# Expert weights loaded once per layer into SBUF, and copied tile by tile into the ring by VectorE

## The reference

```python
gate_logits = x @ Wg + bg
top_vals, top_idx = jax.lax.top_k(gate_logits, TOP_K)      # TOP_K = 2 of 8
...
h = jnp.einsum('td,edh->eth', xf, W0) + b0[:, None, :]      # gated: 128 -> 512, twice
g = jax.nn.silu(jnp.einsum('td,edh->eth', xf, W1) + b1[:, None, :])
y = jnp.einsum('eth,ehd->etd', h * g, W2) + b2[:, None, :]  # 512 -> 128
...
    h = jax.nn.gelu(flat @ W1[e] + b1[e], approximate=False)   # ungated: 128 -> 512, once
    out = out + combine[:, e:e + 1] * (h @ W2[e] + b2[e])
```

## Time and profile before

| | |
|---|---|
| median of three runs | 1117.88 us (1116.94 to 1121.6) |
| the profiled execution's own time | 1118.18 us |
| its span, first to last instruction | 1116.4 us |
| mean granted TensorE clock | 0.863 of full speed |
| busy: PE, PEld, DVE, ACT, POOL | 797.7, 680.7, 538.7, 445.3, 433.3 us |
| chain that ended last | PE 58%, DVE 24%, issue 7%, DMA 4%, ACT 3%, POOL 3% |
| DMA queue q1 (SyncE's and the other hardware queues) | 134.03 MB |

### The profile page before, as it was taken

The page is one execution under the profiler, slowest core; times in us unless marked ns, Lnnn a source line. Parts: engine busy times, 40 slices in busy tenths (PEclk is TensorE's granted clock), DMA queues, the critical chain, the costliest instruction groups (busy, mean ns, idle before and its releaser), DMA issues.

```text
span 1116.4 us, 17251 instructions
## 1 busy us (share of the span) xinstructions
PE 797.7 (71%) x5220; PEld 680.7 (61%) x5220; DVE 538.7 (48%) x1633; ACT 445.3 (40%) x1259; POOL 433.3 (39%) x448
## 2 busy tenths in 40 slices
PE   0579997378989865899974767774177877777750
PEld 0479997267777645798973566664034555666650
DVE  4734444777656537344447521113889543310117
ACT  0045554144445320455550145553087331265540
POOL 1256663022222210565631066663453210466631
PEclk9999999698989985799995579997598885699995
DMA  4559985362513003598954247775000011477752
GB/s 110 131 177 293 291 271 180 95 152 55 124 42 82 2 9 121 179 291 279 276 174 132 94 114 213 211 207 144 1 0 1 1 30 35 136 212 211 210 162 65
DMA packets 79082, 153.77 MB, mean 138 GB/s; under 512 B 11082, under 2 KB 54035, under 8 KB 78992
## 3 DMA queue, kind: packets, MB, share of 16 engines
q1 hardware_dynamic: 69008, 134.03, 40.6%
q0 software_dynamic: 9984, 18.65, 6.1%
HBM read 134.21 MB, written 20.25 MB: 138 GB/s over the span
## 4 chain that ended last, share of the span: by engine, by line
PE 58%; DVE 24%; issue 7%; DMA 4%; ACT 3%; POOL 3%; SPq 1%; another core or an unknown queue 0%; POOLq 0%; ACTq 0%; DVEq 0%
PE bank L521 14%; PE bank L512 12%; PE bank L509 8%; PE bank L945 2%; DVE stats L281 2%; PE bank L528 2%; PE bank L460 2%; PE bank L935 2%; DVE oh_b L623 2%; PE bank L497 2%; DVE sh_tok L675 2%; PE bank L1270 2%; DVE x_tok L675 2%; PE bank L908 1%; PE bank L477 1%
## 5 line engine op out<-in xcount | busy, mean ns | idle before, releaser
L512 PE MATMUL bank<-xt,weights 128*128 128x128 f32 x1248 | 249.8, 283 | 27.5 <-ACT xt L411 16.6
L521 PE MATMUL bank<-hid,weights 128*128 128x128 f32 x1248 | 245.1, 279 | 11.0 <-ACT hid L422 8.2
L348 POOL DMA_INDIRECT xg<-xn_rows,gidx x156 | 153.1, 982 | 238.7 <-DVE gidx L629 129.9
L512 PEld LDWEIGHTS bank<-xt,weights 128*128 128x128 f32 x1248 | 196.5, 199 | 33.9 <-ACT xt L411 20.3
L521 PEld LDWEIGHTS bank<-hid,weights 128*128 128x128 f32 x1248 | 191.1, 194 | 15.3 <-ACT hid L422 9.5
L355 POOL DMA_INDIRECT y_rows<-yo,sidx x156 | 157.1, 1007 | 91.8 <-issue 56.3
L650 DVE SCALAR_TENSOR_TENSOR hid<-bank,weights,act_ring 128x128 f32<-128x128 f32 x312 | 108.9, 349 | 139.5 <-ACT act_ring L422 83.2
L422 ACT ACTIVATE act_ring<-bank,weights 128x128 f32<-128x128 f32 x312 | 115.8, 371 | 111.1 <-PE bank L512 96.5
L657 DVE COPY yo<-bank 128x128 f32<-128x128 f32 x156 | 44.6, 286 | 213.2 <-remote 127.6
L422 ACT ACTIVATE hid<-bank,weights 128x128 f32<-128x128 f32 x312 | 110.6, 372 | 79.8 <-PE bank L521 51.1
L509 PE MATMUL bank<-xt,weights 128*128 128x128 f32 x624 | 128.8, 289 | 5.8 <-issue 2.5
(11 more groups left out here) (220 smaller groups left out, 1341.8 us busy)
## 6 DMA issues: line engine op xcount, KB each, us to landing
weights<-glu_pack SPq DMA_DIRECT2D x78, 772.5 KB
weights<-mlp_pack SPq DMA_DIRECT2D x78, 514.5 KB
v_sb<-v_rows SPq DMA_DIRECT2D x48, 180.0 KB, 6.5
y_in<-y_rows SPq DMA_DIRECT2D x32, 256.0 KB, 5.0
xn_rows<-xm_tok SPq DMA_DIRECT2D x16, 256.0 KB, 2.2
v_rows<-vd SPq DMA_DIRECT2D x16, 256.0 KB, 2.8
xg<-xn_rows,gidx POOLq DMA_INDIRECT x156
y_rows<-yo,sidx POOLq DMA_INDIRECT x156
```

What stands on the lines that cost most here:

```text
L348: pool.indirect_dma_start(out=xg[:, slot, :], out_offset=None, in_=xn_dram.ap()[:, :], in_offset=bass.IndirectOffsetOnAxis(ap=gidx[:, j:j ...
L512: nc.tensor.matmul(banks[k % 4][:, 0:TS], wt[:, slot, o:o + P], xt[:, j % 2, :], start=True, stop=True).then_inc(sem(st + "_up"), 1)
L521: nc.tensor.matmul(YD[j % 2], wt[:, j % WSLOTS, o:o + P], hid[:, k % 4, :], start=c == 0, stop=c == HC - 1).then_inc(sem(st + "_dn"), 1)
```

## The change

At a layer's front SyncE now issues eight DMAs that load all eight experts' sets into a new SBUF tensor `all_w`. They are behind the four stores of `xn_rows` and wait for nothing else. SyncE no longer reads `te_i`. VectorE has a generator `tile_weights(j)`: it waits for the ring slot, reads the expert into a register of its own, and copies the set out of `all_w` in pieces of 512, 512 and 521 columns (gated) or 512 and 517 (ungated), one piece per step. The ring has four slots in place of five. Three sets are copied before the tile loop; in the loop, tile j carries the copies of tile j+3, one piece behind each `chunk(j, c)`. TensorE waits for one semaphore `_tile_w`.

```diff
--- before.py
+++ after.py
@@ -24,7 +24,7 @@
 NTILE = (2 * NT * P + E * (TS - 1)) // TS
 NA = -(-NTILE // 2) * 2
 SLOTS_BASE = 2 * NT * P
-WSLOTS, XSLOTS, PIECES, LAG = 5, 6, 4, 3
+WSLOTS, XSLOTS, PIECES, LAG = 4, 6, 4, 3
 BEHIND = 3
 
 
@@ -78,9 +78,7 @@
     if kind in ("glu", "mlp"):
         per = {"_up": HC * NTILE, "_act": HC * NTILE, "_hid": HC * NTILE, "_dn": HC * NTILE, "_gT": NTILE, "_xt": NTILE,
                "_ysb": NTILE, "_yT": NTILE, "_yo": NTILE, "_xn_out": 16 * NBLK, "_logits": 1, "_scattered": 16 * NTILE, "_incl": 1, "_offs": 1,
-               "_te": 1, "_onehot": PIECES, "_table": 1, "_idx": 1, "_gap": 1, "_tanh": 1}
-        for i in range(WSLOTS):
-            per[f"_w_in{i}"] = 16 * turns_of(WSLOTS, i)
+               "_te": 1, "_weights_in": 16 * E, "_tile_w": NTILE, "_onehot": PIECES, "_table": 1, "_idx": 1, "_gap": 1, "_tanh": 1}
         for i in range(XSLOTS):
             per[f"_xg_in{i}"] = 16 * turns_of(XSLOTS, i)
         for b in range(NBLK):
@@ -205,9 +203,9 @@
             with ExitStack() as place:
                 return [place.enter_context(nc.sbuf_tensor(n, s, d)) for n, s, d in tensors]
 
-        xm_tok, xT_sb, wt, eq_a, oh_a, oh_b, xg, xt, act_ring, hid, yt, yo, y_in, sh_tok, mix_w, cv_w = shared_place(
-            ("xm_tok", [P, NT, D], F32), ("xT_sb", [P, NBLK, BC], F32), ("weights", [P, WSLOTS, GLU_COLS], F32),
+        eq_a, oh_a, oh_b, xm_tok, xT_sb, all_w, xg, xt, act_ring, hid, yt, yo, y_in, sh_tok, mix_w, cv_w = shared_place(
             ("eq_a", [P, 2 * NT, NA], F32), ("oh_a", [P, 2 * NT, NA], R32), ("oh_b", [P, 2 * NT, P], R32),
+            ("xm_tok", [P, NT, D], F32), ("xT_sb", [P, NBLK, BC], F32), ("all_w", [P, E * GLU_COLS], F32),
             ("xg", [P, XSLOTS, D], F32), ("xt", [P, 2, TS], F32), ("act_ring", [P, 4, TS], F32),
             ("hid", [P, 4, TS], F32), ("yt", [P, 2, TS], F32), ("yo", [P, NTILE, D], F32),
             ("y_in", [P, 2, NT, D], F32), ("sh_tok", [P, NT, D], F32),
@@ -220,6 +218,7 @@
             ("scores", [P, 2, 8, KEYS], F32), ("probs", [P, 4, 8, KEYS], F32), ("probsT", [P, 2, 4 * ROWS], F32),
             ("rowmax", [P, 2, 8], F32), ("rowsum", [P, 2, 8], F32), ("rowinv", [P, 4, 8], F32), ("wo_T", [P, BC], F32))
 
+        wt, = shared_place(("weights", [P, WSLOTS, GLU_COLS], F32))
         zero_rows = y_in[:, 1, 0:2, :].rearrange("p t d -> p (t d)")
         attn_raw = y_in[:, 0, :, :].rearrange("p t d -> p (t d)")[:, 0:OCOL]
         rwkv_in = y_in[:, 0, :, :].rearrange("p t d -> p (t d)")[:, 0:RWKV_COLS]
@@ -299,14 +298,12 @@
             moments(v, st, name, src)
             return normalise(v, st, name, src, n, 0, dst)
 
-        def tile_weights(sp, n, st, m, j):
-            slot = j % WSLOTS
+        def all_weights(sp, n, st, m):
+
             pack = glu_pack if m.gated else mlp_pack
-            if j >= WSLOTS:
-                sp.wait_ge(sem(st + "_ysb"), st.at("_ysb", j - WSLOTS + 1))
-            e = sp.value_load(te_i[0:1, j:j + 1], min_val=0, max_val=E - 1)
-            sp.dma_start(wt[:, slot, 0:m.cols], pack[:, bass.ds(e * m.cols, m.cols)]).then_inc(
-                sem(st + f"_w_in{slot}"), 16)
+            for e in range(E):
+                cols = slice(e * m.cols, (e + 1) * m.cols)
+                sp.dma_start(all_w[:, cols], pack[:, cols]).then_inc(sem(st + "_weights_in"), 16)
 
         def zero_values(sp):
             sp.wait_ge(sem("zero_rows_set"), 1)
@@ -321,13 +318,11 @@
                 sp.wait_ge(sem(st + "_in_norm"), st.at("_in_norm", b + 1))
                 sp.dma_start(xn_dram.ap().rearrange("(t p) d -> p t d", p=P)[:, TPB * b:TPB * (b + 1), :],
                              xm_tok[:, TPB * b:TPB * (b + 1), :]).then_inc(sem(st + "_xn_out"), 16)
+            all_weights(sp, n, st, m)
             if feeds(n):
                 rwkv_raw(sp)
             if n == 0:
                 zero_values(sp)
-            sp.wait_ge(sem(st + "_te"), st.at("_te", 1))
-            for j in range(NTILE):
-                tile_weights(sp, n, st, m, j)
             sp.wait_ge(sem(st + "_scattered"), st.at("_scattered", 16 * NTILE))
             if n == 0:
                 sp.wait_ge(sem("attn_w_ready"), 2 * OCOL // 512)
@@ -500,7 +495,7 @@
                 k, slot = HC * j + c, j % WSLOTS
                 if c == 0:
                     pe.wait_ge(sem(st + "_xt"), st.at("_xt", j + 1))
-                    pe.wait_ge(sem(st + f"_w_in{slot}"), st.at(f"_w_in{slot}", 16 * (j // WSLOTS + 1)))
+                    pe.wait_ge(sem(st + "_tile_w"), st.at("_tile_w", j + 1))
                 if k >= 4:
                     pe.wait_ge(sem(st + "_hid"), st.at("_hid", k - 3))
                 elif not m.gated:
@@ -640,6 +635,27 @@
                     link(nc.vector.tensor_tensor(x_tok[:, tb, :], x_tok[:, tb, :],
                                                  half_beta[:, :].unsqueeze(1).broadcast_to([P, TPB, D]), ALU.add))
 
+            def tile_weights(j):
+
+                slot = j % WSLOTS
+                if j >= WSLOTS:
+                    v.wait_ge(sem(st + "_ysb"), st.at("_ysb", j - WSLOTS + 1))
+                e = v.value_load(te_i[0:1, j:j + 1], min_val=0, max_val=E - 1)
+                for i in range(m.ups + 1):
+                    first, last = 512 * i, m.cols if i == m.ups else 512 * (i + 1)
+                    ins = nc.vector.tensor_copy(wt[:, slot, first:last],
+                                                all_w[:, bass.ds(e * m.cols + first, last - first)])
+                    if i < m.ups:
+                        yield
+                ins.then_inc(sem(st + "_tile_w"), 1)
+                yield
+
+            v.wait_ge(sem(st + "_te"), st.at("_te", 1))
+            v.wait_ge(sem(st + "_weights_in"), st.at("_weights_in", 16 * E))
+            for j in range(WSLOTS - 1):
+                for _ in tile_weights(j):
+                    pass
+
             def chunk(j, c):
                 if not m.gated:
                     return
@@ -657,10 +673,12 @@
                 nc.vector.tensor_copy(yo[:, j, :], YO).then_inc(sem(st + "_yo"), 1)
 
             for j in range(NTILE):
+                ahead = tile_weights(j + WSLOTS - 1) if j + WSLOTS - 1 < NTILE else iter(())
                 for c in range(HC):
                     chunk(j, c)
                     if c == 1 and j >= 2:
                         tile_out(j - 2)
+                    next(ahead, None)
                 if feeds(n) and 8 <= j < 8 + 11:
                     rwkv_weight(j - 8)
             tile_out(NTILE - 2)
```

## The result

| | before | after |
|---|---|---|
| median | 1118.39 us (1116.94 to 1121.6, 4 runs) | 1207.98 us (1207.53 to 1213.56, 4 runs) |
| span of the profiled execution | 1116.4 us | 1211.8 us |
| mean granted clock | 0.863 | 0.864 |

The ratio is 1.0803, 95% interval 1.0766 to 1.0839: +90 us where +116 was forecast. A fifth execution of the changed kernel took 1206.1 us. The profiled one, at 1213.56, is the longest of the five, 5.6 us over the median.

The account below looks back on a forecast made before the run. Gated loops were taken as bound by TensorE, ungated ones by a round trip that gathers lengthen by 1.1 us. Gated +77, ungated +36 and fronts +3 made +116 on 1118, so 1234 us, range 1158 to 1325.

Parts of the forecast that it names:

- the wait closes a ring: In the tile loops VectorE's wait for the previous tile's yt closes a ring with TensorE: +77 us gated, +36 ungated.
- VectorE's own load, gated: VectorE's work per gated tile, four `hid`, yo, register load and three copies: 3.64 us against a period of 3.18.
- Rival C: Tile loops: only VectorE's 3.64 us load counts gated, ungated ring stays at 3.15; +40, 1158 us; chance 0.10.
- The gated ring: Gated loops: last `hid`, `down`, yt, register load, copies, next tile's last `hid`; 4.06 us, taken as 4.25, +77 us.
- The allowance for gathers: Extra per tile while gathers run, added to the rings: 0.19 us gated, 0.45 ungated.
- rival A: Granted clock falls to half in the ungated loops: +40 to +79, 1274 to 1313 us; chance 0.15.
- Ungated ring over yo: Ungated loops: register load, copy, yo, transpose to last `down`, yt; 3.15 us, taken as 3.60 against 3.10, +36 us.
- Register load 0.70, copy 0.34, 521 columns no dearer: On VectorE's queue a register load takes 0.70 us and each copy 0.34, the 521-column piece included.
- The fronts, +3, and the DMA traffic, 0: Layer fronts: loads covered, first ungated set late, +3 us for two layers; weight DMAs that go away are worth 0.
- B: Port shared by VectorE and GpSimd holds copies that meet indirect DMAs: +72, 1306 us; chance 0.13.
- D: DMA traffic stretches the round trip while gathers run, and its end makes the loops faster: 1027 us; chance 0.04.
- The signs named: Profile: 390 copies near 0.43 us, VectorE about 705 us, q1 about 52 MB, yt 4.0 to 4.5 and 3.2 to 4.0.

Follow-up runs that it names:

- an earlier load: Changed kernel with VectorE's register load moved ahead of the ring wait: 1157.94 us, ratio 1.0356.
- a later place: Changed kernel, still four slots, with all copies of tile j+3 issued behind tile j's last `hid`: 1124.86 us, ratio 1.0063.
- one load more: Changed kernel with a second, unused register load per tile on VectorE behind the wait: 1296.44 us, ratio 1.1592.
- the narrow copies: Changed kernel with every copy in the tile loop cut to 64 columns, output changed: 1180.09 us, ratio 1.0579.
- SyncE run: Changed kernel with SyncE filling the four-slot ring by DMA out of `all_w`, no VectorE copies or register loads: 1130.04 us, ratio 1.0120.
- four slots: Kernel before the change with four ring slots instead of five: 1130.28 us, ratio 1.0125.
- thin loads: Kernel before the change with weight loads behind the first five tiles cut to 16 columns, output changed: 1116.66 us, ratio 0.9999.

## Why the prediction was right in kind, and 26 us too high

**That the wait closes a ring:** right. Four edits show it: an earlier load (-50 us), one slot more (-85), a later place (-83), one load more (+88).

**VectorE's own load, gated, 3.64 us, "over the period of 3.18, whatever else holds":** wrong. The 0.43 was the distance of `hid` in the earlier trace rows that each still had to wait for ScalarE's `act_ring`; back to back a `hid` gives way after 0.26. The load is 2.98, and with the ring broken the gated period is 3.12 to 3.13. Rival C at 1158 rested on the 3.64 and has no basis.

**The gated ring:** the sum was nearly right, the route was not. This is the step that failed, though the total hides it: I closed it over the last `hid` of tile j. By measured slots that route is 0.53 + 1.13 (yt and load) + 0.34 + 0.26 + 0.20 + 0.34 + 0.26 + 0.34 + 0.35 = 3.75 us, and so it never binds. The ring that does goes over the second `hid`, the one behind the first copy, and then over sixteen TensorE records, from its `down` to the tile's last one: 4.00. I had asked which `hid` TensorE waits for last in the program, not which it comes to first with the longest queue behind it. That 4.06 stood against 4.00 is luck, two errors that cancel: 0.17 too much on each of two `hid` slots, and a route 0.25 too short; the narrow copies told them apart, 28 us against 64.

**The allowance for gathers, 0.19 gated and 0.45 ungated:** wrong, and more than the whole miss: it put in 72 x (0.19 + 0.45) = 46 us, and 26 are missed. The last gather of the first loop is out at 195.05 and its next periods are 4.01, 4.00 and 4.00 us, as while gathers ran; in the third loop, behind the last gather at 829.69, they are 3.28, 3.28 and 3.27. A ring longer than the old round trip takes nothing more from the gathers. Without it, by the sum of 4.06 and 3.15 against 3.18 and 3.10, the forecast would have been 72 x (0.88 + 0.05) + 3 = +70; by the measured periods it is 72 x (0.82 + 0.17) = +71. Both are some 20 short of the loops' +91. Up to 6.5 of these are the low clock at the start of three loops (rival A below). Most of the rest, about 13 us, is the tail: the forecast took the ring against periods with gathers, but the last tiles before ran at 2.90 and 2.00, and the changed kernel's ring takes that from them too. By means of whole loops, tail and clock included, it is (3.95 - 3.08) x 76 + (3.27 - 2.93) x 76 = 92 us. My allowances thus stood in, by their size, for what I had left out, and the 26 us too high are the difference.

**Ungated ring over yo:** right in route. Term by term, yt and load 1.10 forecast and 1.13 measured, copy 0.34 and 0.34, the rest 1.71 and 1.81.

**Register load 0.70, copy 0.34, 521 columns no dearer:** right. 0.72 to 0.73, 0.34, and 424 ns against 428. The Trainium skill, page "DMA: Bandwidth & Descriptors", section "🔬 Latency and other measured facts", gives `tensor_load` a floor of about 600 ns. The load's own row here is 298 ns at its shortest and 304 at the median, below that floor, and only with its range check and address behind it does it come to 0.72.

**The fronts, +3, and the DMA traffic, 0:** no cost of the loads is seen (SyncE run against four slots, 1130.04 and 1130.28 us), and the traffic costs nothing (thin loads). The ungated layers' 3 us are not to be seen: the stretches with those fronts changed by +0.8 and -1.7.

**Not priced at all: the slot.** The change also takes one slot of five. With weights by DMA that costs 12 to 16 us. With VectorE filling the ring its cost is another one, and far larger: it moves the wait one tile nearer. Of the 90 us, 85 are in that one number.

**Rivals.** A: the clock fell, but only at the start of three loops, here in the third:

```profile
730.90:737.80 6.90, 5.82 (x27) 5.58 (x28) 1.93 (x6) 2.68 (x8) 2.99 (x3) 0.51 0.10 29
```

That is the lower level, 1.2 GHz. The tiles there took 4.36, 4.31 and 4.10 us for 3.27, and with the first tiles of the other loops (5.71 and 4.36; 5.46, for 4.00) it is 6.5 us at most. The rest of every loop had the full clock, so the ring, once it ran, did not bring the clock down. The 20 records of a tile in the forecast should be 18, since each transpose is one record: 1.96 us, 54% of 3.60. B: the copies' mean was 0.426 us and two indirect DMAs 1009 and 1022 ns, before 1007 and 982 ns. Of the copies 217 overlapped an indirect DMA, with a mean of 0.429 us against 0.423 for the other 173; ten took over 0.45, the longest 0.651. With five slots the indirect DMAs had means of 1045 and 1051 ns, so something is left of B, but under 0.1 us each. By the Trainium skill, page "SBUF — State Buffer", section "SBUF: two separate sides", one of the two should stand still while the other has the pair; 390 copies beside 312 indirect DMAs do not bear this out. Beside a 128x512 tensor operation of GpSimd VectorE did stand still in the kernel before, as the page has it: the first of the four at 838.43 in the earlier trace rows was followed after 1.21 us, as that operation ended, and the others after 0.26. The forecast's 1.5 us for four by the `hid` pace should be 1.64 by its own 0.43, or 1.12 by 0.26. D is refuted above.

**The signs named.** Copies 390, mean 0.426 us; queue q1 52.31 MB; yt 4.00 and 3.27 us apart; the gated wait put down to yt; TensorE idle 0.83 us ahead of its `down` in the gated tile read above: as named. Missed: VectorE's busy time is 659.0 us and not 705, since the last 0.09 us of a copy lie under the next instruction's start; the granted clock in the third loop is 0.97.

**Outcome.** None of these kernels beats the one before. The nearest with copies on VectorE is five slots, 4 us behind it.

## What to carry to other kernels

When a wait is put onto an engine that feeds a third one, look for the ring: start at the event waited for, go over the first instruction queued behind the wait that someone else needs, and then over all that is queued behind *that* on the next engine. Add up every such route: here the earliest one closed the ring (4.00 us), not the last (3.75). Then ask for the cheapest place where the event is long past: a slot more, or the end of the step. Here either took back over 80 of 90 us, and what is left for the work itself is 4 to 7. Take the mean of a whole loop, its tail included, when you multiply a difference of periods by a count.

## What the chip showed that I had not expected

- A VectorE copy of 64 columns lasts 0.20 us and the next instruction starts 0.10 to 0.11 behind it; at 512 columns 0.43 and 0.34. In a queue, cost an instruction by the next one's start.
- The front's loads of 772.5 and 514.5 KB landed 4.0 to 14.3 us after their issue, and the SyncE kernel, which has them, is no longer outside the loops than the kernels without. In the loops, the thin loads took q1 from 134.03 to 45.53 MB and no mean period fell (3.09 and 2.95 us for 3.08 and 2.93).
- In the kernel before VectorE stood still beside a 128x512 tensor operation of GpSimd (1.21 us for 0.26), but in the changed one its copies were hardly held beside GpSimd's indirect DMAs (0.429 us for 0.423).
- The 1.1 us by which gathers lengthened an ungated tile before are gone once another ring is the longer one: 3.27 us with gathers and 3.28 without. Why they lengthen the short round trip was not tried, only that it is not the weights' traffic (thin loads).
- A register load on VectorE's queue is 0.72 us in which nothing behind it starts, twice the 0.34 of a 512-column copy; a second one behind it adds 0.63.
